# Opening stage as a pipeline over tiles, and a middle stage in which ScalarE and TensorE finish a pair before the next

## The reference

```python
h = relu(layernorm(x))
# layer 0, two steps
S = adj + I;  Rf = S / rowsum(S);  Rb = S / colsum(S)[:, None]
Xf = Xb = Xa = h
for s in (0, 1):
    logits = (Xa @ W1) @ W2 @ (Xa @ W3).T
    A = softmax(logits, kept to the smallest set of entries that holds 0.9 of the row)
    Xf, Xb, Xa = Rf @ Xf, Rb @ Xb, A @ Xa
    Z += Xf @ U1[s] + Xb @ U2[s] + Xa @ U3[s]
x = x + layernorm(h + Z) * gamma + beta
# layer 1
h = relu(layernorm(x))
e = (h @ edge_w) @ (h @ edge_w).T, masked where adj is 0
out = x + adj * softmax(h @ node_w over nodes) * softmax(e) @ (h @ weight) + bias
```

## Time and profile before

| | |
|---|---|
| median of 3 runs | 4305.14 us (4302.59 to 4307.82) |
| the profiled execution | 4310.23 us, span of its instructions 4308.4 us |
| opening, to DVE's last instruction in it | 185.35 us |
| stage between attention and edges | 3413.16 to 3647.41 us |
| busy over the span | DVE 85%, PE 72%, ACT 69%, POOL 7% |

### The profile page before, as it was taken

One profiled execution on the slowest core, in us unless ns is written; L12 is line 12 of the kernel. 1 busy time (PEld: TensorE's weight loads), 2 busy tenths in 40 slices (PEclk: granted clock), 3 DMA queues, 4 the chain that ended last, 5 costly groups with the idle time before them and its releaser, 6 DMA issues. The chain is left out here.

```text
span 4308.4 us, 41843 instructions
## 1 busy us (share of the span) xinstructions
PE 3101.3 (72%) x14280; PEld 2139.9 (50%) x14330; DVE 3669.6 (85%) x4935; ACT 2984.8 (69%) x3947; POOL 321.9 (7%) x319
## 2 busy tenths in 40 slices
PE   2646787877878785558786877968777344988888
PEld 2335565665656664424353443534444233566666
DVE  3399999999999999599999999999999543666766
ACT  1299999999999971499999999899980111222222
POOL 0000000000000000000000000000000132322322
PEclk9968988988989997879898988989888667999999
DMA  0111212212212121311111111111111231122221
GB/s 34 42 52 56 90 49 73 76 63 82 69 61 82 57 81 52 125 33 41 46 32 37 41 36 42 32 37 43 36 43 31 82 97 64 67 91 74 74 92 45
DMA packets 108035, 254.24 MB, mean 59 GB/s; under 512 B 11888, under 2 KB 47792, under 8 KB 104368
## 3 DMA queue, kind: packets, MB, share of 16 engines
q1 hardware_dynamic: 89104, 224.32, 16.2%
q10 hardware_dynamic: 18720, 27.27, 1.7%
HBM read 217.47 MB, written 34.08 MB: 58 GB/s over the span
## 5 line engine op out<-in xcount | busy, mean ns | idle before, releaser
L619 DVE SCALAR_TENSOR_TENSOR s_dump<-s_rows,s_mid 128x3327 bf16<-128x3327 f32 x684 | 2518.1, 3681 | 0.7 <-issue 0.2
L569 ACT ACTIVATE s_adump<-s_rows,s_mid 128x3327 bf16<-128x3327 f32 (+1 forms) x304 | 933.6, 3071 | 9.9
L574 ACT ACTIVATE s_adump<-s_rows,s_mid 128x3327 bf16<-128x3327 f32 (+1 forms) x304 | 930.0, 3059 | 5.9 <-ACT s_sx_out L480 3.1
L767 PE MATMUL bank<-x,s_slab 128*128 128x512 f32 x1352 | 615.5, 608 | 0.0
L810 PE MATMUL bank<-hb,s_wT 128*128 128x256 f32 x1352 | 359.8, 411 | 121.1 <-ACT s_wT L458 120.9
L810 PE MATMUL bank<-xab,s_wT 128*128 128x256 f32 x1352 | 351.2, 404 | 114.9 <-ACT s_wT L458 114.9
L767 PEld LDWEIGHTS bank<-x,s_slab 128*128 128x128 f32 x1352 | 265.4, 197 | 314.9 <-issue 308.8
L1200 ACT ACTIVATE e_wh<-bank 128x512 f16<-128x512 f32 (+1 forms) x182 | 102.5, 565 | 448.2 <-PE bank L1299 448.1
L458 ACT ACTIVATE s_wT<-bank 128x512 f32<-128x512 f32 (+1 forms) x364 | 201.2, 553 | 287.5 <-PE bank L799 287.5
L799 PE MATMUL bank<-ident,s_rows 128*128 128x128 f32 x1352 | 227.7, 295 | 181.0 <-DVE s_rows L639 181.0
L746 PE MATMUL bank<-kh,qs 128*128 128x512 f16 (+1 forms) x364 | 145.4, 399 | 282.2 <-DVE s_rows L598 271.7
(11 more groups left out here) (175 smaller groups left out, 4657.1 us busy)
## 6 DMA issues: line engine op xcount, KB each, us to landing
s_slab<-adjT_dram SPq DMA_DIRECT2D x104, 448.0 KB, 3.8
e_adj<-adjR_dram SPq DMA_DIRECT2D x26, 1664.0 KB, 7.4
s_slab<-adjT_dram SPq DMA_DIRECT2D x104, 384.0 KB, 3.6
strip<-adjR_dram SPq DMA_DIRECT2D x52, 448.0 KB, 3.5
strip<-adjR_dram SPq DMA_DIRECT2D x52, 384.0 KB, 3.3
su_d<-s_su_out ACTq DMA_DIRECT2D x26, 256.0 KB, 2.0
zu_d<-s_zu_out ACTq DMA_DIRECT2D x26, 256.0 KB, 2.0
sx_d<-s_sx_out ACTq DMA_DIRECT2D x26, 256.0 KB, 2.0
```

Of the source, the lines that this page charges most:

```text
L569: nc.scalar.activation(adump[:], row(g, 2), ACT.Sign, bias=st(mid, g, 2), accum_out=cnt[:]).then_inc(S["a_eval"], 1)
L574: nc.scalar.activation(adump[:], row(g, 2), ACT.Relu, bias=st(mid, g, 2), accum_out=gap[:]).then_inc(S["a_eval"], 1)
L619: nc.vector.scalar_tensor_tensor(out=dump[:], in0=row(g, r), scalar=st(mid, g, r), in1=row(g, r), op0=ALU.is_gt, op1=ALU.mult, accum_out=s ...
L767: ins = nc.tensor.matmul(acc, slab[:, i % NSLAB, j - PIECES[p], :], s_op[:, j, 0:SN], start=False, stop=(j == NT - 1))
```

## The change

Opening. x is loaded in seven batches of tiles (2, then six of 4), the first two ahead of the small weights. DVE makes the mean and variance of each tile with bn_stats and bn_aggr; POOL makes the inverse roots of a batch with pow and two Newton steps, and -mean / root; ACT writes hb in one activation with scale and bias per row. The loops are unrolled and staggered: PE turns tile t and projects t - 2; ACT takes positive t, columns t - 1, high parts t - 3. The turned tile has three PSUM banks, the projections four, q16 four cells; POOL takes over the copy of the high half of the queries. The stage has 25 semaphores where it had 14.

Middle stage. ACT takes positive, columns and high parts of one pair before it goes to the next; PE turns both tiles of a pair and then projects both. DVE's extra increments of `moments` (skip_moments) go, and POOL's waits count accordingly.

```diff
+    BATCH = (0, 2, 6, 10, 14, 18, 22, 26)
+    psW, psX, psK = psum[0], psum[1:4], psum[4:8]
...
+            def load(i):
+                tiles = slice(BATCH[i], BATCH[i + 1])
+                sp.dma_start(xs[:, tiles, :], x[:, tiles, :]).then_inc(x_in[i], 16)
+
+            load(0)
+            load(1)
+            sp.dma_start(ident[:], ident_in).then_inc(S["ident_in"], 16)
+            sp.dma_start(w1t[:], W1T).then_inc(S["w12_in"], 16)
+            sp.dma_start(w2[:], W2).then_inc(S["w12_in"], 16)
             for half in range(2):
                 sp.dma_start(wk2[:, :, half * DA:(half + 1) * DA],
+                             W3.rearrange("(c p) n -> p c n", p=P)).then_inc(S["wk_in"], 16)
+            for i in range(2, NB):
+                load(i)
+
+        @block.gpsimd
+        def _(pool):
+            own = Own(pool, S["own_pool"])
+
+            def inverse_roots(i):
+                k = slice(BATCH[i], BATCH[i + 1])
+                pool.wait_ge(S["moments"], BATCH[i + 1])
+                r, v, w = inv[:, k], ve[:, k], cor[:, k]
+                own.link(nc.gpsimd.tensor_scalar(v, mv[:, k, 1], EPS, None, ALU.add))
+                own.link(nc.gpsimd.tensor_tensor(r, v, power[:, k], ALU.pow))
+                for _ in range(2):
+                    own.link(nc.gpsimd.tensor_tensor(w, r, r, ALU.mult))
+                    own.link(nc.gpsimd.tensor_tensor(w, w, v, ALU.mult))
+                    own.link(nc.gpsimd.tensor_scalar(w, w, -0.5, 1.5, ALU.mult, ALU.add))
+                    own.link(nc.gpsimd.tensor_tensor(r, r, w, ALU.mult))
+                own.link(nc.gpsimd.tensor_tensor(nmr[:, k], mv[:, k, 0], r, ALU.mult))
+                nc.gpsimd.tensor_scalar(nmr[:, k], nmr[:, k], -1.0, None, ALU.mult).then_inc(S["roots_ready"], 1)
+
+            def keep(t):
+                pool.wait_ge(S["q_high"], t + 1)
+                nc.gpsimd.tensor_copy(qs[0:DA, t * P:(t + 1) * P], q16[0:DA, t % 4, :]).then_inc(S["q_kept"], 1)
+
+            own.link(nc.gpsimd.memset(power[:], -0.5))
+            for i in range(NB + 2):
+                if i < NB:
+                    inverse_roots(i)
+                if i >= 2:
+                    for t in range(BATCH[i - 2], BATCH[i - 1]):
+                        keep(t)
 
         @block.vector
+            def statistics(i):
+                dve.wait_ge(x_in[i], 16)
+                for t in range(BATCH[i], BATCH[i + 1]):
+                    own.link(nc.vector.bn_stats(stat[:, t], xs[:, t]))
+                for t in range(BATCH[i], BATCH[i + 1]):
+                    nc.vector.bn_aggr(mv[:, t], stat[:, t]).then_inc(S["moments"], 1)
+
+            def low_parts(t):
+                cols = slice(t * P, (t + 1) * P)
+                dve.wait_ge(S["k_high"], t + 1)
+                dve.wait_ge(S["q_high"], t + 1)
+                nc.vector.tensor_tensor(kl2[:, cols], psK[t % 4][:, 0:P], kh2[:, cols], ALU.subtract)
+                nc.vector.tensor_tensor(qs[DA:P, cols], psK[t % 4][DA:P, P:2 * P], q16[DA:P, t % 4, :], ALU.subtract).then_inc(S["qk_low"], 1)
+
+            statistics(0)
+            statistics(1)
+            nc.vector.memset(hb[:, :, D:D + 1], 1.0).then_inc(S["consts"], 1)
+            nc.vector.memset(hb[:, :, D + 1:HROW], 0.0).then_inc(S["consts"], 1)
+            for i in range(NB):
+                if i + 2 < NB:
+                    statistics(i + 2)
+                for t in range(BATCH[i], BATCH[i + 1]):
+                    low_parts(t)
 
         @block.scalar
+            def positive(t):
+                batch = next(i for i in range(NB) if BATCH[i + 1] > t)
+                act.wait_ge(S["roots_ready"], batch + 1)
+                nc.scalar.activation(hb[:, t, 0:D], xs[:, t], ACT.Relu, scale=inv[:, t:t + 1], bias=nmr[:, t:t + 1]).then_inc(S["h_ready"], 1)
+
+            def columns(t):
+                act.wait_ge(S["xt_done"], t + 1)
+                if t >= 2:
+                    act.wait_ge(S["qk_done"], t - 1)
+                nc.scalar.activation(xT[:, t % 2], psX[t % 3][:, 0:D].rearrange("p (c n) -> p c n", c=KC), ACT.Copy).then_inc(S["xt_ready"], 1)
+
+            def high_parts(t):
+                act.wait_ge(S["qk_done"], t + 1)
+                nc.scalar.activation(kh2[:, t * P:(t + 1) * P], psK[t % 4][:, 0:P], ACT.Copy).then_inc(S["k_high"], 1)
+                if t >= 4:
+                    act.wait_ge(S["qk_low"], t - 3)
+                    act.wait_ge(S["q_kept"], t - 3)
+                nc.scalar.activation(q16[:, t % 4, :], psK[t % 4][:, P:2 * P], ACT.Copy).then_inc(S["q_high"], 1)
+
+            act.wait_ge(S["w12_done"], 1)
             for half in range(2):
                 nc.scalar.activation(wq2[:, :, half * DA:(half + 1) * DA],
+                                     psW[:, 0:KC * DA].rearrange("p (c n) -> p c n", c=KC), ACT.Copy).then_inc(S["w12_ready"], 1)
+            for t in range(NT + 3):
+                if t < NT:
+                    positive(t)
+                if 1 <= t <= NT:
+                    columns(t - 1)
+                if t >= 3:
+                    high_parts(t - 3)
 
         @block.tensor
+            def turn(t):
+                pe.wait_ge(S["h_ready"], t + 1)
+                if t >= 3:
+                    pe.wait_ge(S["xt_ready"], t - 2)
+                for k in range(KC):
+                    last = nc.tensor.transpose(psX[t % 3][:, k * P:(k + 1) * P], hb[:, t, k * P:(k + 1) * P], ident[:])
+                last.then_inc(S["xt_done"], 1)
+
+            def project(t):
+                pe.wait_ge(S["xt_ready"], t + 1)
+                if t >= 4:
+                    pe.wait_ge(S["qk_low"], t - 3)
+                for n, w in enumerate((wk2, wq2)):
+                    for k in range(KC):
+                        last = nc.tensor.matmul(psK[t % 4][:, n * P:(n + 1) * P], w[:, k, :], xT[:, t % 2, k, :], start=(k == 0), stop=(k == KC - 1))
+                last.then_inc(S["qk_done"], 1)
+
+            pe.wait_ge(S["w12_in"], 32)
             for k in range(KC):
+                last = nc.tensor.matmul(psW[:, k * DA:(k + 1) * DA], w1t[:, k * P:(k + 1) * P], w2[:], start=True, stop=True)
+            last.then_inc(S["w12_done"], 1)
+            pe.wait_ge(S["ident_in"], 16)
+            for t in range(NT + 2):
+                if t < NT:
+                    turn(t)
+                if t == 2:
+                    pe.wait_ge(S["wk_in"], 32)
+                    pe.wait_ge(S["w12_ready"], 2)
+                if t >= 2:
+                    project(t - 2)
 
 
...
 
             def inverse_roots(i):
                 k = i % CELLS
-                pool.wait_ge(S["moments"], 4 * (i + 1))
+                pool.wait_ge(S["moments"], 4 * i + 2 if i < NPAIR else 4 * NPAIR)
                 if i >= CELLS:
                     pool.wait_ge(S["h2_ready"], 2 * (i - CELLS))
                 r, v, w = inv[:, k], ve[:, k], cor[:, k]
@@ -1003,10 +1042,6 @@
                 for k in range(2):
                     nc.vector.bn_aggr(mv[:, i % CELLS, w + k], stat[:, w + k]).then_inc(S["moments"], 1)
 
-            def skip_moments(w):
-                for k in range(2):
-                    dve.sem_inc(S["moments"], 1)
-
             def normalize(t):
                 i, k = divmod(t, 2)
                 u, m, cell = t % 4, t % 6, i % CELLS
@@ -1038,8 +1073,6 @@
                     dve.wait_ge(S["y_ready"], 2 * (i + 1))
                     statistics(y, 2 * i % 4, 0)
                     moments(i, 0)
-                elif i == NPAIR:
-                    skip_moments(0)
                 if 1 <= i <= NPAIR:
                     dve.wait_ge(S["roots_ready"], i)
                     for k in range(2):
@@ -1047,8 +1080,6 @@
                     dve.wait_ge(S["x1_ready"], 2 * i)
                     statistics(x1, 2 * (i - 1) % 6, 2)
                     moments(i, 2)
-                elif i == 0:
-                    skip_moments(2)
 
         @block.scalar
         def _(act):
@@ -1073,16 +1104,13 @@
                 nc.scalar.activation(hth[:, :, cols], psR[t % 4][:, 0:D].rearrange("p (c n) -> p c n", c=KC), ACT.Copy).then_inc(S["hi_ready"], 1)
                 nc.scalar.activation(sup[:, t, 0:D], psR[t % 4][:, D:2 * D], ACT.Copy).then_inc(S["hi_ready"], 1)
 
-            for i in range(NPAIR + 1):
-                if i < NPAIR:
-                    for k in range(2):
-                        positive(2 * i + k)
-                if i >= 1:
-                    for k in range(2):
-                        high_parts(2 * (i - 1) + k)
-                if i < NPAIR:
-                    for k in range(2):
-                        columns(2 * i + k)
+            for i in range(NPAIR):
+                for k in range(2):
+                    positive(2 * i + k)
+                for k in range(2):
+                    columns(2 * i + k)
+                for k in range(2):
+                    high_parts(2 * i + k)
 
         @block.tensor
         def _(pe):
@@ -1109,11 +1137,11 @@
```

(55 more changed lines are left out.)

62 lines of the change are left out of this document (8 added, 54 removed).

## The result

| | before | after |
|---|---|---|
| median of 4 runs, the two kernels side by side | 4304.01 us (4302.59 to 4307.82) | 4097.58 us (4096.98 to 4103.59) |
| profiled execution / its span | 4310.23 / 4308.4 us | 4103.59 / 4101.8 us |
| next stage's first DVE instruction | 186.94 us | 55.11 us |
| stage between attention and edges, to the first DVE instruction behind it | 237.3 us | 168.4 us |
| the rest (two steps and edges) | 3884.2 us | 3878.3 us |

The ratio is 0.9522, 95% interval 0.9506 to 0.9539. 4107 us was forecast, and 4097.6 came out. By stages of the profiled executions: -131.8 us in the opening (forecast -125.3), -68.9 in the middle stage (forecast -72.5), and -5.9 in stages that the diff doesn't touch.

The account below looks back on a forecast made before the run. DVE's bisection was taken as the largest part, untouched; chains of waits bound the two changed stages. Opening -126.3, clearing +1.0 and middle stage -72.5 gave -197.8: 4112.4 us profiled, 4107 us median, 8-in-10 range 4087 to 4143.

Parts of the forecast that it names:

- Start: Opening: first load at about 3.9 us, first positive at 9.5, third at 13.9.
- Pace: Opening: 1.65 us per tile, with two tiles at 2.5 until the clock rises.
- two-tile round trip: Opening: positive t, turn, project t-2, columns and high parts, positive t+2 take 3.0 us at the higher clock level.
- The longer path: Opening: DVE's statistics, POOL's roots and keeps, ScalarE's q16 ring; 7.7 us plus 0.3 against five tiles, 1.6 per tile.
- Clock: Opening: TensorE, at its lower level before, won't pause and should rise; projections at 275 ns instead of 421.
- End and clearing: Opening: 5.4 us after the last positive; clearing eleven more semaphores adds 1.0 us.
- The chain of a pair: Middle stage: from a pair's positives to its last high part, 8.75 us; 7.0 with TensorE at the higher level.
- two-pair tie: Middle stage: with LAG = 3, roots, chain, second low part and the rest span two pairs: 21.2 us, 10.6 per pair.
- (a): Rival: TensorE stays at its lower level in the opening, perhaps also the middle; 4125 to 4140 us, chance 0.17.
- (b): Rival: the middle stage gains nothing because DVE's in-order wait finds another late partner; 4179 us, chance 0.06.
- (c): Rival: POOL, on both stages' chains, is slowed to 1.51 us per operation beside DVE; 4400 us, chance 0.02.
- (d): Rival: the steps between get slower or shift by as much as is won; chance 0.03 together with unknown.

Follow-up runs that it names:

- e8: e7 with three xT cells instead of two and ScalarE's high parts one tile later in the opening; 4090.39 us, ratio 0.9492.
- e9: e7 with opening batches of 2, 4, 8, 8, 4 tiles instead of 2 and six of 4; 4090.96 us, ratio 0.9498.
- e7: e4 with eight q16 cells instead of four in the opening; 4090.72 us, ratio 0.9499.
- e3: The changed kernel without the opening's stagger: ScalarE and TensorE finish tile t before tile t+1; 4170.22 us, ratio 0.9684.
- e2: The kernel before with only the middle stage changed, its opening as it was; 4236.38 us, ratio 0.9839.
- e6: e4 with POOL's two side sums of the middle stage over 4 of 256 columns, so its output differs; 4067.89 us, ratio 0.9443.
- e4: The changed kernel with LAG = 4 instead of 3: DVE takes a pair's low parts one iteration later in the middle stage; 4085.89 us, ratio 0.9491.

## Why the prediction was right, point by point

- **Start.** First statistics at 3.9, first positive at 9.5, third at 13.9; measured 3.48, 8.79, 13.12. The mechanism held; the first load came 0.4 us earlier, and the roots of a batch of two took 4.0 us (4.84 to 8.79) and not 4.4, because pow on 128x2 lasts 0.74 us and not 1.04.
- **Pace.** This is the term that was mis-sized most. Forecast were 1.65 us per tile behind two at 2.5; the 23 steps from the third to the last positive took 47.76 - 13.12 = 34.64 us where the forecast has 39.65. The two-tile round trip is 2.69 us (20.56 to 23.25), not 3.0. The longer path, over statistics, roots and keeps, was named with 1.6 and measures 1.46: POOL's batches of roots start at 22.16, 27.55, 33.88 and 39.26, 5.39 and 6.33 us apart in turn, and before the third of these POOL waits 1.17 us for DVE's statistics (timeline of the changed kernel):

```profile
33.88 0.23 POOL L185 TENSOR_SCALAR h_ve<-h_mv 128x4 f32<-128x4 f32 x1 [1.17 <-DVE h_mv L216]
```

  e8 shows that this path, and not the round trip, sets the average: with the round trip cut to 1.08 the end came no earlier (52.91 us). The two are close: in e9, where this path is shorter, tiles come at the round trip's 1.34 behind the stall. Its last link, the q16 ring, is not the one that matters (e7).
- **Clock.** That the opening would rise after the first tiles held (five us at 421 ns, then 275). e3 shows what the rise hangs on: with the same instructions in the order of a chain TensorE stays at 1.2 GHz.
- **End and clearing.** Last positive to last low part 4.96 us against 5.4; the gap grew by 0.8 against 1.0. The next stage's first DVE instruction, forecast near 62 with "right from 56 to 80", came at 55.1, so just outside its own sign: all terms of the opening erred to the same side.
- **Middle stage.** The chain of a pair was forecast as 8.75 us from the lower level and 7.0 from the higher: 8.72 and 6.89. The two-pair tie was forecast as 21.2 us and is 22.2. 0.75 of this 1.0 is that POOL's roots take 5.07 us (aggregate's end 3367.60 to 3372.67) and not 4.32: the small POOL operations last 0.36 to 0.44 instead of 0.20 where DVE's two-input sums run beside them. The forecast had the collision on DVE's side only. Over the four ties from 3328.32 to 3417.03 (88.7 us against 84.8) that is 3.9 us, and the stage is 3.6 us longer than forecast (in e2, the same code, 1.3). The sign "pairs 9.2 to 11.5 apart" holds for the mean of 11.1 only: every second distance is 12.9.
- **The rule on the shared access.** The Trainium skill, "SBUF — State Buffer", "Who interferes with whom", says that a DVE instruction with two SBUF inputs contends with a POOL instruction that reads SBUF, over ports that are an exclusive lock. From this I took full blocking, +2.9 us a pair and -65 for the stage; the page gives no price for this case. The trace agrees that they contend, with at most 0.94 for 0.48 on DVE; e6 gives 1.6 us a pair. Four such DVE operations and four of POOL's sums, end to end, would take 4 x 0.48 + 4 x 0.73 = 4.8 us, and DVE was through in 3.5 (e4), so they overlap in part. -68.9 lies between that -65 and my -72.5. That both sides are lengthened (POOL's sum 0.73 to 0.92 in the changed kernel, its small operations 0.20 to 0.44) is what neither sum had.
- **Rivals.** (a) is not in the changed kernel and is in e3. (b) is wrong: DVE's wait did find another partner, the tie of two pairs that the forecast had, but at 11.1 and not at 17 us. (c) is wrong: POOL's copies of the opening last 0.28 to 0.29 us, all 26, and its small operations other than pow 0.20 to 0.25; the copies of 1.51 in the earlier trace rows stood beside reads of 3.68 us. (d): nothing outside got slower.
- **The 5.9 us in other stages.** Over the eleven kernels measured behind the one before, the rest scatters between 3876.9 and 3887.8 us with no order in what was changed, 3884.2 in the kernel before. So part of the 206 us may be such scatter; that the change makes the other stages shorter isn't shown, and what moves them wasn't tried.
- **What was luck.** The profiled execution came out 8.8 us below its forecast of 4112.4. The opening's terms account for 6.5 of it and the middle stage for -3.6; the other 5.9 are in stages for which the forecast had no term. The mechanisms were right; that the total is so close is in part two errors of opposite sign.

Not tried alone: the edit of the counters in the middle stage.

## What to carry to other kernels

Where no engine is busy for much more than half of a stage, write down the chain of one tile and ask which link is tied to another tile's only by the order of the code: e3 shows that this order, not the work, was worth 68 of 132 us in the opening, and in the middle stage it was the 69 (together with the edit of the counters). Staggering paid twice on TensorE here, once for the overlap and once for the clock, which rose behind five us of work without a pause (421 to 275 ns). When one tie is cut, the next one stands close behind (11.1, 9.8 and, with the side sums cut short, 8.2 us per pair in turn), so work out the next before another buffer or a deeper stagger is spent on it: e7 and e8 bought at most 1 us.
